# Graph layers on one core: scatter one-hots of the attention layer prebuilt in the propagation, and its combining step in float16

## The chip, the cores and the metric

The kernel runs on one core of one Trainium2 chip. The metric is the device time of one execution in microseconds (us); lower is better. An engine is named as the profile names it: PE (TensorE), PEld (its weight loads), DVE (VectorE), ACT (ScalarE), POOL (GpSimd), SP (SyncE, which here only issues DMAs).

## What is computed

Four graph layers, each on the layer norm and relu of the running `x` (3125 nodes of 64 features), over the same 53125 edges sorted by `dst`:

```python
h = relu(layernorm(x)); x = x + L0(h)   # K = 10 times: h' = 0.9 * norm * segsum(h[src] * norm[src]) + 0.1 * h0
h = relu(layernorm(x)); x = x + L1(h)   # attention per edge: 4 heads, exp(clip(q.k)), normalised per node, times v
h = relu(layernorm(x)); x = x + L2(h)   # segsum(h[src] * edge_weight) / deg, two 64x64 products
h = relu(layernorm(x)); x = x + L3(h)   # segsum(h[src] * sigmoid(edge_attr_64 @ ps_w)) * ci
```

## The kernel before, in words

The nodes lie as 25 tiles of 125 (`T`, `P`). A **flag** computed at run time picks the fast path, which all runs here take.

**Start.** DVE computes for each edge its tiles, its rank and its slot; meanwhile PE turns the 13.6 MB of edge features (L1285) and forms the logits of layer 3 from them (L1298), in 17 pieces. When the flag is known DVE sorts the edges into slots (L964 to L968, one round per tile, with PE L1341). At the end PE turns the 17 columns of logits back (L1361), ACT takes their sigmoid into `wpa` (L600, semaphore `pa_ready`), and POOL begins to place the pairs (edge weight, sigmoid) into `w_table` in HBM, with 425 indirect DMAs (L489). The table is read back (SP L425) before layer 2, after all placing is done (`w_placed`).

**Adjacency.** 25 rounds: DVE makes bf16 one-hots of sources and targets (L998, L1001), PE multiplies them (L1387), ACT copies the counts into `adj`, the 3125 x 3125 matrix in float16, which fills the arena. The target one-hots go to `ohd_table` in HBM for layers 2 and 3.

**Propagation (L0).** Ten iterations. `hl` holds each node's values as a float16 high part and a float16 low part, 128 columns. An iteration has seven chunks (`NCH`), six of 500 nodes and one of 125. For a chunk PE runs 25 matmuls, one per source tile (L1424), into the chunk's own PSUM bank; ACT copies the bank into `part` (L629, float32); PE *combines* the chunk one place behind (L1410): per tile of 125 nodes a float32 matmul, issued as two instructions, with the 125 columns of `part` as weights and `pair` (two identities on top of each other) as the moving operand. That adds high and low and turns them back to nodes on partitions. All combined tiles go through PSUM bank 7. DVE then makes the next `h`, high and low parts, in four instructions (L1074, L1077, L1079, L1081). Semaphores: `mains` (bank full), `mains_taken` (bank copied), `combined`, `sums_read` (bank 7 read by L1074), `hl_ready`. The combining of the seventh chunk stands inside the first chunk of the next iteration, after 12 of its matmuls.

**Edge layers (L1, L2, L3).** Software pipelines over 25 tiles plus four steps, each engine with its own order, written out in `edge_layer` and stepped by `tile_steps`. SP loads the source slots of a tile, spread to all partitions, into `rowbc` (L369, from `slot_rows`); DVE compares them with the lane number (L791) and so makes one-hots for the gather; PE gathers (L1237, L1242), the values are weighted, and PE scatters with one-hots of the other side (L1255). In the attention layer `rowbc` has two loads per tile, one for sources and one for targets, and one buffer for each. One step `s` of it on DVE is: L804 (products q times k, tile s-2), L791 (one-hot, tile s), L809 (logits, s-2), L791 (second one-hot, s), L815 (clip), L818 (low part of the message, s-3), L823 (weighted values, s-2), and L797, `ohd_of`: the scatter one-hots of tile s-2. On ACT it is: six of the 13 row copies (L528, tile s-1), the exponential (L536, after L815), seven more row copies, the high part (L546) and the sums (L564). PE's step is 13 groups of gathers for tile s-1, with the 26 scatter matmuls of tile s-4 behind the sixth group. Layers 2 and 3 read their scatter one-hots from `ohd_table` (L373) instead of computing them. The read waits until the scatter two tiles earlier has left its buffer, and stands in SP's one queue behind the step's loads of `rowbc`:

```python
if 2 in on and p != "l1":
    sp.wait_ge(S[p + "_scat"], d - 1)
    sp.dma_start(ohd_words[:, par], ohd_table[...])
```

## Time and profile before

| | us |
|---|---|
| Median of 3 runs | 1431.04 (1430.93 to 1431.52) |
| The profiled execution, its own time | 1421.67 |
| its span | 1420.0 |
| PE busy, share of the span | 1038.1, 73% |
| DVE busy | 958.2, 67% |
| POOL busy | 715.1, 50% |
| ACT busy | 566.7, 40% |
| Mean granted clock of PE | 0.826 |

The busy shares are means over stages with different limits. Stages of the span, by their first and last instructions: start and flag to 94 us, sorting to 205, adjacency to 335, propagation to 721, its residual and the next layer norm and products to 779, attention to 1067, layer 2 to 1275, layer 3 to the end.

### The profile page before, as it was taken

To read this page: it belongs to the slowest core of one execution; us is meant where nothing else is said; L and a number is where in the kernel's file an instruction comes from. 1 tells how busy PE (TensorE), PEld (TensorE's weight loads), DVE (VectorE), ACT (ScalarE), POOL (GpSimd) and SP (SyncE) were. 2 spreads that over 40 slices of the span, in tenths; PEclk is the share of its full clock that TensorE was granted. 3 is DMA by queue.
4 is the path that set the end of the run, shared out by engine and by line. 5 is a ranking of instruction groups with operands and counts; after the bars stand their busy time and mean duration, and the time that the engine had idled before them with its cause. 6 is when DMAs were issued, how large, how long until landed. Compare 5 with 4: busy or idle time off the path is not lost.

```text
span 1420.0 us, 32164 instructions
## 1 busy us (share of the span) xinstructions
PE 1038.1 (73%) x12016; PEld 802.3 (57%) x12016; DVE 958.2 (67%) x1175; ACT 566.7 (40%) x1381; POOL 715.1 (50%) x444
## 2 busy tenths in 40 slices
PE   4956567877999999999934677767762766646764
PEld 3635457763555555555524677766662666545664
DVE  7885779993223223223255999999997788558875
ACT  1321127662010101101113766666651777417773
POOL 1000018888787878787888899999940000000000
PEclk9977655567999999999967878888765999759997
DMA  7642006551000000000012544444411889418894
GB/s 153 137 102 70 23 14 208 180 190 30 2 2 2 1 1 1 1 1 2 2 51 52 192 145 145 161 153 156 156 67 50 330 321 344 159 42 328 326 334 147
DMA packets 61492, 169.86 MB, mean 120 GB/s; under 512 B 32531, under 2 KB 33331, under 8 KB 61437
## 3 DMA queue, kind: packets, MB, share of 16 engines
q1 hardware_dynamic: 45371, 154.59, 30.5%
q10 hardware_dynamic: 2465, 13.60, 4.1%
q0 software_dynamic: 13600, 0.92, 3.5%
q8 instruction: 36, 0.59, 0.2%
q14 instruction: 20, 0.16, 0.0%
HBM read 144.28 MB, written 24.33 MB: 119 GB/s over the span
## 4 chain that ended last, share of the span: by engine, by line
PE 39%; DVE 31%; issue 15%; DMA 9%; ACT 3%; DVEq 2%; SPq 1%; ACTq 0%
PE ps L1424 24%; DMA hl_room<-slot_rows 7%; PE ps L1410 4%; DVE arena L809 3%; DVE base_room L804 3%; PE ps L1237 3%; PE ps L1298 2%; PE ps L1255 2%; DVE hl_room L998 2%; DMA hl_room<-in_edge_attr_dram 2%; DVE arena L886 2%; PE ps L1285 2%; DVE h_room L823 2%; DVE arena L823 1%; ACT arena L561 1%
## 5 line engine op out<-in xcount | busy, mean ns | idle before, releaser
L489 POOL DMA_INDIRECT w_table<-wpa,slot_i x425 | 710.4, 1672 | 329.3 <-ACT wpa L600 200.1
L1237 PE MATMUL ps<-arena 125*128 125x64 f16 (+1 forms) x3900 | 257.2, 218 | 165.7 <-ACT arena L528 75.6
L1424 PE MATMUL ps<-arena,hl_room 125*128 125x500 f16 (+1 forms) x1750 | 345.1, 353 | 9.1 <-DVEq L1062 9.1
L1237 PEld LDWEIGHTS ps<-arena 125*128 125x128 bf16 x3900 | 189.8, 105 | 181.8 <-ACT arena L528 74.6
L1424 PEld LDWEIGHTS ps<-arena,hl_room 125*128 125x128 f16 x1750 | 161.6, 100 | 169.7 <-issue 13.2
L1074 DVE TENSOR_TENSOR h_room<-ps,coef 125x256 f32<-125x256 f32 (+1 forms) x70 | 27.7, 396 | 271.5 <-PE ps L1410 271.5
L629 ACT ACTIVATE part_room<-ps 128x500 f32<-128x500 f32 (+1 forms) x70 | 38.0, 543 | 349.7 <-PE ps L1424 349.7
L1255 PE MATMUL ps<-arena 128*128 128x128 f16 (+1 forms) x1950 | 142.7, 238 | 21.6 <-DVE arena L818 9.8
L1242 PE MATMUL ps<-arena 125*128 (+1 forms) x1300 | 149.6, 214 | 0.0
L1255 PEld LDWEIGHTS ps<-arena 128*128 128x128 bf16 x1950 | 131.2, 108 | 24.3 <-issue 22.0
L791 DVE TENSOR_SCALAR arena<-hl_room,lane 125x3328 bf16<-125x3328 bf16 x100 | 108.3, 1086 | 48.8 <-DMA hl_room<-slot_rows 47.5
L528 ACT ACTIVATE arena<-ps 128x384 f32<-128x384 f32 x325 | 131.0, 504 | 10.1 <-PE ps L1242 8.0
L1242 PEld LDWEIGHTS ps<-arena 125*128 125x128 bf16 x1300 | 124.5, 116 | 0.4
L554 ACT ACTIVATE arena<-ps,part_room 128x64 f32<-128x64 f32 x500 | 107.3, 343 | 16.4 <-PE ps L1237 16.3
L561 ACT ACTIVATE arena<-arena 128x1664 f16<-128x1664 f32 x50 | 79.5, 1591 | 61.9 <-DVE arena L841 56.0
L832 DVE TENSOR_TENSOR arena<-arena 128x1664 f16<-128x1664 f32 x50 | 94.4, 1888 | 14.6 <-ACT arena L561 14.5
L613 ACT ACTIVATE arena<-ps 125x500 f32 x150 | 79.7, 591 | 35.6 <-PE ps L1378 21.0
L582 ACT ACTIVATE part_room<-ps 128x500 f32<-128x500 f32 x68 | 34.6, 509 | 136.7 <-PE ps L1285 136.6
L1410 PEld LDWEIGHTS ps<-pair,part_room 128*125 128x125 f32 x500 | 64.7, 189 | 8.9 <-issue 0.7
L1298 PE MATMUL ps<-part_room,psw 128*26 128x125 f32 (+1 forms) x442 | 65.7, 291 | 1.0 <-ACT arena L574 0.8
L841 DVE TENSOR_TENSOR arena<-ps,part_room 128x512 f32<-128x512 f32 x100 | 64.2, 682 | 0.6 <-PE ps L1237 0.5
L1285 PE MATMUL ps<-ident,hl_room 125*128 125x125 f32 (+1 forms) x221 | 44.5, 326 | 26.7 <-DMA hl_room<-in_edge_attr_dram 18.8
(244 smaller groups left out, 1336.1 us busy)
## 6 DMA issues: line engine op xcount, KB each, us to landing
hl_room<-slot_rows SPq DMA_DIRECT2D x100, 832.0 KB, 5.6
arena<-ohd_table SPq DMA_DIRECT2D x50, 832.0 KB, 5.8
hl_room<-in_edge_attr_dram ACTq DMA_DIRECT2D x17, 750.0 KB
w_table<-wpa,slot_i POOLq DMA_INDIRECT x425
ohd_table<-hl_room SPq DMA_DIRECT2D x13, 448.0 KB, 2.6
ohd_table<-base_room SPq DMA_DIRECT2D x12, 448.0 KB, 2.6
ohd_table<-hl_room SPq DMA_DIRECT2D x13, 384.0 KB
ohd_table<-base_room SPq DMA_DIRECT2D x12, 384.0 KB
```

The lines of the kernel that those rows point to most:

```text
L489: pool.indirect_dma_start(w_table, bass.IndirectOffsetOnAxis(slot_i[:, u:u + 1], 0), wpa[:, u], None).then_inc(S[f"w_out{g % 2}"], 16)
L528: act.activation(G1[:, 1 - par, 2 * m:2 * m + 2, :], ps[:, m % RING, 0:2 * 3 * D].rearrange("p (c f) -> p c f", c=2), ACT.Copy).then_inc(S ...
L554: last = act.activation(msgf[:, par, c, :], ps[:, m, k * D:(k + 1) * D], ACT.Copy, scale=wsl[:, bass.ds((s - 2) * C + c, 1), 0 if p == "l2 ...
L561: act.activation(msg2[:, par, :, 0:D], msgf[:, par], ACT.Copy).then_inc(S[p + "_high"], 1)
L791: done = vec.tensor_scalar(ohT[:, par, e], rowbc[0:P, e if p == "l1" else par], lane[0:P, :], None, ALU.is_equal)
L832: vec.tensor_tensor(msg2[:, 1 - par, :, D:], msgf[:, 1 - par], msg2[:, 1 - par, :, 0:D], ALU.subtract).then_inc(S[p + "_low"], 1)
L1237: last = pe.matmul(ps[:, m % RING, o:o + b - a], ohT[:, par, 0, k * L:(k + 1) * L], rhs, start=(i == 0), stop=(i == 1))
L1242: last = pe.matmul(ps[:, m % RING, o + 2 * D:o + w], ohT[:, par, 1, k * L:(k + 1) * L], rhs, start=(i == 0), stop=(i == 1))
L1255: last = pe.matmul(ps[:, RING + par, 0:m1], ohd[par][:, k // 2, :, k % 2], msg1[:, par, k, :] if p == "l1" else msg2[:, par, k, :], start= ...
L1298: last = pe.matmul(ps[0:CJ + 1, 7, 0:P], psw2[0:w, at:at + CJ + 1], eaT[0:w, g % 2, k * P:(k + 1) * P], start=(block == 0), stop=(block == ...
L1410: last = pe.matmul(ps[0:P, 7, k * D:(k + 1) * D], part[:, odd, k * P:(k + 1) * P], pair[:, :], start=True, stop=True)
L1424: last = pe.matmul(ps[:, c, 0:w], hl[0:P, u, s, :], adj[:, s, c * CH * P:c * CH * P + w], start=(s == 0), stop=(s == T - 1))
```

## The change

- **Scatter one-hots of the attention layer**: DVE no longer makes them in that layer (`ohd_of` is gone). It makes them during the propagation, 50 halves, one behind each of the chunks 1 to 5 of every iteration, and SP writes them to a new table `ohs_table` in HBM. The attention layer reads them from there as layers 2 and 3 do. Their two buffers take the room of `xs` (the running `x`), so `x` is read again from HBM once the last half is written.
- **Turning in float16**: ACT writes the high part of a chunk's sums, scaled by 1/4096, as float16, DVE writes the low part (one instruction more per chunk, `low_sums`), and PE combines with two float16 matmuls per tile on 128 weight columns.
- **Weights placed from the flag on**: the logits of the first 250 of 425 edge columns are turned back and put through the sigmoid before the flag is known; POOL may place those at once, and the other 175 when the rest is ready.

```diff
@@ -30,6 +30,7 @@
+PSCALE = 4096.0
...
+        ohs_table = nc.dram_tensor("ohs_table", [T, L, CP * OW * 2], BF16).ap()
-        xs = sb("xs", [P, T, D])
+        xs_room = sb("xs_room", [L, KG[0] * OW])
+        xs = xs_room[0:P, 0:T * D].rearrange("p (t f) -> p t f", t=T)
-        part = part_room[:, 0:2 * CH * P].rearrange("p (a n) -> p a n", a=2)
+        part = part_room[:, 0:2 * CH * L].bitcast(F16).rearrange("p (a e n) -> p a e n", a=2, e=2)
-        pair = sb("pair", [L, D])
+        pair = sb("pair", [L, D], F16)
-        iota_h = sb("iota_h", [L, Q], F16)
+        iota_h = sb("iota_h", [L, OW], F16)
...
+        EARLY = EA_FLAG // 4
...
-                    if 2 in on and p != "l1":
+                    if 2 in on:
                         sp.wait_ge(S[p + "_scat"], d - 1)
-                        sp.dma_start(ohd_words[:, par], ohd_table[bass.ds(d - 2, 1)].rearrange("t p x -> p (t x)")
+                        sp.dma_start(ohd_words[:, par], (ohs_table if p == "l1" else ohd_table)[bass.ds(d - 2, 1)].rearrange("t p x -> p (t x)")
                                      ).then_inc(S[p + f"_ohd{par}"], 16)
                 tile_steps(sp, body)
                 sp.wait_ge(S[p + "_ohT"], T + free)
@@ -413,6 +421,16 @@
                     sp.wait_ge(S["table_ready"], n + 1)
                     sp.dma_start(g_table.rearrange("(t p) f -> p t f", p=P), h[:, :, :]).then_inc(S["table_in"], 16)
             with sp.If(way < 1):
+                with sp.Fori(0, T) as t:
+                    for half in range(2):
+                        a = sum(KG[:half]) * OW
+                        sp.wait_ge(S["ohs_made"], t * 2 + (half + 1))
+                        sp.dma_start(ohs_table[bass.ds(t, 1), :, a:a + KG[half] * OW].rearrange("t p x -> p (t x)"), ohs_words[half]
+                                     ).then_inc(S[f"ohs_out{half}"], 16)
+                for half in range(2):
+                    sp.wait_ge(S[f"ohs_out{half}"], 16 * (T + 1))
+                for a, b in SPLIT:
+                    sp.dma_start(xs[a:b, :, :], x.rearrange("(t p) f -> p t f", p=P)[a:b]).then_inc(S["x_back"], 16)
                 sp.wait_ge(S["rows_out"], 96)
                 sp.wait_ge(S["l0_done"], 1)
                 load_rows("l1", (1, 2))
@@ -472,17 +490,20 @@
...
                 pool.wait_ge(S["pa_ready"], 1)
                 pool.wait_ge(S["w_cleared"], 16)
+                assert EARLY * CJ % SU == 0
 
                 for g in range(J // SU):
+                    if g * SU == EARLY * CJ:
+                        pool.wait_ge(S["pa_ready"], 2)
...
             load_features(1)
             turned_features(0, EA_FLAG)
+            turned_logits(EARLY - 1)
+            act.wait_ge(S["z_back"], 1)
+            act.activation(wpa[:, 0:EARLY * CJ, 1], ps[0:P, 4, 0:EARLY * CJ], ACT.Sigmoid).then_inc(S["pa_ready"], 1)
             way = path(act)
             with act.If(way < 1):
                 act.activation(rep2[:, :, :], iota_h[:, 0:OW].unsqueeze(2).to_broadcast([L, OW, 2]), ACT.Copy).then_inc(S["rep_ready"], 1)
...
-                act.wait_ge(S["z_back"], 1)
-                act.activation(wpa[:, :, 1], ps[0:P, 5, 0:J], ACT.Sigmoid).then_inc(S["pa_ready"], 1)
+                act.wait_ge(S["z_back"], 2)
+                act.activation(wpa[:, EARLY * CJ:, 1], ps[0:P, 5, EARLY * CJ:J], ACT.Sigmoid).then_inc(S["pa_ready"], 1)
...
-                            act.activation(part[:, n % 2, 0:w], ps[:, c, 0:w], ACT.Copy).then_inc(S["mains_taken"], 1)
+                            act.activation(part[:, n % 2, 0, 0:w], ps[:, c, 0:w], ACT.Copy, scale=1 / PSCALE).then_inc(S["part_high"], 1)
                 act.wait_ge(S["rows_out"], 96)
...
                     done.then_inc(S[p + "_ohT" if e == ends - 1 else "l1_first"], 1)
-
-                def ohd_of(s, par):
-
-                    vec.wait_ge(S[p + "_scat"], s - 1)
-                    vec.tensor_tensor(ohd[par], nodes(C), pairs(sls_h[:, bass.ds((s - 2) * C, C)], C),
-                                      ALU.is_equal).then_inc(S[p + "_ohd"], 1)
...
@@ -1058,30 +1074,66 @@
                 one_hots_kept(vec)
                 fast(vec.tensor_copy(hl[0:P, 0, :, 0:D], h[:, :, :]))
                 fast(vec.tensor_tensor(hl[0:P, 0, :, D:], h[:, :, :], hl[0:P, 0, :, 0:D], ALU.subtract))
-                fast(vec.tensor_scalar(coef[:, :], rdeg[:, :], 1 - ALPHA, None, ALU.mult))
+                fast(vec.tensor_scalar(coef[:, :], rdeg[:, :], (1 - ALPHA) * PSCALE, None, ALU.mult))
+                vec.wait_ge(S["rows_out"], 96)
+                fast(vec.memset(part[:, :, :, CH * P:], 0.0))
+                vec.sem_inc(S["mains_taken"], NCH)
                 vec.sem_inc(S["hl_ready"], NCH)
                 vec.sem_inc(S["sums_read"], 1)
                 vec.wait_ge(S["base_ready"], 1)
-                with vec.Fori(0, K0 // 2) as i:
-                    for u in range(2):
-                        for c in range(NCH):
-                            n = u * NCH + c
-                            k = min(CH, T - CH * c)
-                            t = slice(CH * c, CH * c + k)
-                            turned = ps[0:P, 7, 0:k * D].rearrange("p (t f) -> p t f", t=k)
-                            vec.wait_ge(S["combined"], i * (2 * NCH) + (n + 3))
-                            vec.tensor_tensor(h[:, t, :], turned, coef[:, t].unsqueeze(2).to_broadcast([P, k, D]), ALU.mult
-                                              ).then_inc(S["sums_read"], 1)
...
+
+                def low_sums(i, n):
+                    c = n % NCH
+                    w = min(CH, T - CH * c) * P
+                    vec.wait_ge(S["part_high"], i * (2 * NCH) + (n + 1))
+                    vec.scalar_tensor_tensor(part[:, n % 2, 1, 0:w], ps[:, c, 0:w], 1 / PSCALE, part[:, n % 2, 0, 0:w],
+                                             ALU.mult, ALU.subtract).then_inc(S["mains_taken"], 1)
+
+                def new_nodes(i, n):
+                    u, c = n // NCH, n % NCH
+                    k = min(CH, T - CH * c)
+                    t = slice(CH * c, CH * c + k)
+                    turned = ps[0:P, 7, 0:k * D].rearrange("p (t f) -> p t f", t=k)
+
+                    vec.wait_ge(S["combined"], i * (2 * NCH) + (n + 3))
+                    vec.tensor_tensor(h[:, t, :], turned, coef[:, t].unsqueeze(2).to_broadcast([P, k, D]), ALU.mult
+                                      ).then_inc(S["sums_read"], 1)
+                    vec.wait_ge(S["sums_read"], i * (2 * NCH) + (n + 2))
+                    vec.tensor_tensor(h[:, t, :], h[:, t, :], base[:, t, :], ALU.add).then_inc(S["g_step"], 1)
+                    vec.wait_ge(S["g_step"], i * (4 * NCH) + (2 * n + 1))
+                    vec.tensor_copy(hl[0:P, 1 - u, t, 0:D], h[:, t, :]).then_inc(S["g_step"], 1)
+                    vec.wait_ge(S["g_step"], i * (4 * NCH) + (2 * n + 2))
+                    vec.tensor_tensor(hl[0:P, 1 - u, t, D:], h[:, t, :], hl[0:P, 1 - u, t, 0:D], ALU.subtract
+                                      ).then_inc(S["hl_ready"], 1)
+
+                def scatter_one_hots(t, k):
+                    j, half = k // 2, k % 2
+                    c, n = sum(KG[:half]), KG[half]
+                    vec.wait_ge(S[f"ohs_out{half}"], (t + j) * 16 + 16)
+                    vec.tensor_tensor(ohs_half[half], nodes(n), pairs(sls_h[:, bass.ds((t + j) * C + c, n)], n), ALU.is_equal
+                                      ).then_inc(S["ohs_made"], 1)
+                for half in range(2):
+                    vec.sem_inc(S[f"ohs_out{half}"], 16)
+
+                def two_iterations(i, more):
+                    for n in range(2 * NCH):
+                        u, c = n // NCH, n % NCH
+                        turn = c == NCH - 1
+                        if turn:
+                            new_nodes(i, n)
+                        if more or n + 1 < 2 * NCH:
+                            low_sums(i, n + 1)
+                        if not turn:
+                            new_nodes(i, n)
+                        if 1 <= c <= 5:
+                            scatter_one_hots(i * (T // (K0 // 2)), u * 5 + (c - 1))
+                low_sums(0, 0)
+                with vec.Fori(0, K0 // 2 - 1) as i:
+                    two_iterations(i, True)
+                two_iterations(K0 // 2 - 1, False)
                 vec.wait_ge(S["hl_ready"], (K0 + 1) * NCH)
                 vec.sem_inc(S["l0_done"], 1)
+                vec.wait_ge(S["x_back"], 32)
                 fast(vec.tensor_scalar(coef[:, :], std[:, :], 1.0 / GSCALE, None, ALU.mult))
                 fast(vec.tensor_tensor(h[:, :, :], h[:, :, :], per_node(coef), ALU.mult))
             with vec.Else():
...
+            pe.wait_ge(S["z_turned"], EARLY)
+            for c in range(EARLY):
...
@@ -1407,7 +1461,9 @@
                     pe.wait_ge(S["mains_taken"], n + (NCH + 1))
                     pe.wait_ge(S["sums_read"], n + 1)
                     for k in range(min(CH, T - CH * c)):
-                        last = pe.matmul(ps[0:P, 7, k * D:(k + 1) * D], part[:, odd, k * P:(k + 1) * P], pair[:, :], start=True, stop=True)
+                        for e in range(2):
+                            last = pe.matmul(ps[:, 7, k * D:(k + 1) * D], part[:, odd, e, k * P:k * P + L], pair[:, :],
+                                             start=(e == 0), stop=(e == 1))
                     last.then_inc(S["combined"], 1)
```

Two places where the order of the instructions counts. The first is **SP's queue in the attention layer's loop**, one step of it. Before (`hl_room<-slot_rows` is a load of `rowbc`):

```order
L369 ISA [waits l1_first]
L369 DMA hl_room<-slot_rows 128x3328
L369 ISA [waits l1_ohT]
L369 DMA hl_room<-slot_rows 128x3328
L368 REGISTER_ALU
```

and with the change:

```order
L377 ISA [waits l1_first]
L377 DMA hl_room<-slot_rows 128x3328
L377 ISA [waits l1_ohT]
L377 DMA hl_room<-slot_rows 128x3328
L380 REGISTER_ALU
L381 ISA [waits l1_scat]
L381 DMA arena<-ohs_table 128x3328
```

The next step's first load now stands behind a wait for a scatter on PE and behind a read of the same size.

The second is **DVE's queue in the propagation's loop**, the work behind one chunk of 500 nodes. Before:

```order
L1074 TENSOR_TENSOR h_room<-ps,coef 125x256 [waits combined]
L1077 TENSOR_TENSOR h_room<-h_room,base_room 125x256 [waits sums_read]
L1078 REGISTER_ALU
L1079 CAST hl_room<-h_room 125x4x64 [waits g_step]
L1080 REGISTER_ALU
L1081 TENSOR_TENSOR hl_room<-h_room,hl_room 125x4x64 [waits g_step]
```

and with the change:

```order
L1089 SCALAR_TENSOR_TENSOR part_room<-ps,part_room 128x500 [waits part_high]
L1098 REGISTER_ALU
L1099 TENSOR_TENSOR h_room<-ps,coef 125x256 [waits combined]
L1102 TENSOR_TENSOR h_room<-h_room,base_room 125x256 [waits sums_read]
L1103 REGISTER_ALU
L1104 CAST hl_room<-h_room 125x4x64 [waits g_step]
L1105 REGISTER_ALU
L1106 TENSOR_TENSOR hl_room<-h_room,hl_room 125x4x64 [waits g_step]
L1113 ISA [waits ohs_out1]
L1113 TENSOR_TENSOR xs_room<-rep,sls_h 128x1536
```

The low part of the following chunk stands ahead of the four instructions, and a half of one-hots behind them. Both can hold up what follows them on DVE.

## Rows read from the trace of the kernel before

**Rows 1.** By stretch: us, busy (instructions) by engine, granted clock, DMA share, GB/s

```profile
335.00:721.50 386.50, 384.18 (x2247) 216.41 (x2245) 109.31 (x280) 39.27 (x71) 308.49 (x257) 0.99 0.08 2
779.00:1067.00 288.00, 202.29 (x3200) 195.71 (x3197) 281.93 (x198) 188.00 (x421) 246.78 (x65) 0.79 0.43 146
```

**Rows 2.** Timeline, two chunks of the propagation: start us, us, engine, line, operation

```profile
506.80 5.45 PE L1424 MATMUL ps<-arena,hl_room 125*128 125x500 f16 x25
...
512.91 5.45 PE L1424 MATMUL ps<-arena,hl_room 125*128 125x500 f16 x25
```

**Rows 3.** Timeline, sorting: matmuls on 128 weight columns with 52 moving ones

```profile
170.25 1.16 PE L1341 MATMUL ps<-arena 125*128 125x52 bf16 x34
```

**Rows 4.** Timeline, from the sixth chunk's end into the next iteration

```profile
524.09 1.05 PEld L1410 LDWEIGHTS ps<-pair,part_room 128*125 128x125 f32 x8
...
524.50 0.59 ACT L629 ACTIVATE part_room<-ps 128x500 f32<-128x500 f32 x1 [5.52 <-PE ps L1424]
525.02 1.48 PEld L1424 LDWEIGHTS ps<-arena,hl_room 125*128 125x128 f16 x25
...
525.33 0.42 DVE L1074 TENSOR_TENSOR h_room<-ps,coef 125x256 f32<-125x256 f32 x1 [4.44 <-PE ps L1410]
...
526.57 0.43 DVE L1081 TENSOR_TENSOR hl_room<-h_room,hl_room 125x256 f16<-125x256 f32 x1
```

**Rows 5.** Groups by line: busy us, mean ns of one | idle before

```profile
L841 DVE TENSOR_TENSOR arena<-ps,part_room 128x512 f32<-128x512 f32 x100 | 64.2, 682 | 0.6 <-PE ps L1237 0.5
L998 DVE TENSOR_TENSOR hl_room<-rep,sl_h 128x1792 bf16<-128x1792 f16 (+1 forms) x50 | 50.9, 1018 | 5.2 <-PE ps L1378 2.8 <-ACT wpa L600 2.4
```

**Rows 6.** Timeline, SP at the kernel's end

```profile
1413.37 4.09 SPq L438 DMA_DIRECT2D out_dram<-xs  x2
```

**Rows 7.** The page's DMA part, an issue of one half: KB, us to landing

```profile
ohd_table<-hl_room SPq DMA_DIRECT2D x13, 448.0 KB, 2.6
```

**Rows 8.** Timeline, one step of the attention layer (DVE, ACT, two rows of PE)

```profile
904.29 0.39 PE L1237 MATMUL ps<-arena 125*128 125x128 f16 x2 [1.77 <-ACT arena L528]
...
906.20 1.89 DVE L804 TENSOR_TENSOR base_room<-arena 128x1664 f32<-128x1664 f32 x1
...
908.00 1.08 DVE L791 TENSOR_SCALAR arena<-hl_room,lane 125x3328 bf16<-125x3328 bf16 x1
...
908.13 2.32 PE L1255 MATMUL ps<-arena 128*128 128x136 f16 x26
...
910.80 1.08 DVE L791 TENSOR_SCALAR arena<-hl_room,lane 125x3328 bf16<-125x3328 bf16 x1
...
911.79 0.33 DVE L815 TENSOR_SCALAR arena<-arena,bound 128x104 f32<-128x104 f32 x1
...
912.83 2.76 ACT L528 ACTIVATE arena<-ps 128x384 f32<-128x384 f32 x7
...
915.74 1.89 DVE L797 TENSOR_TENSOR arena<-rep,sls_h 128x3328 bf16<-128x3328 f16 x1
...
917.55 1.89 DVE L804 TENSOR_TENSOR base_room<-arena 128x1664 f32<-128x1664 f32 x1
```

**Rows 9.** DMA issues of 850 to 1000 us: times, KB, median us to landing

```profile
hl_room<-slot_rows SPq DMA_DIRECT2D x26, 832.0 KB, 4.3
```

**Rows 10.** The same of 1120 to 1200 us, in layer 2

```profile
arena<-ohd_table SPq DMA_DIRECT2D x16, 832.0 KB, 5.7
hl_room<-slot_rows SPq DMA_DIRECT2D x16, 832.0 KB, 6.9
```

**Rows 11.** The chain that ended last, at the end of the sorting: start us, us

```profile
202.72 2.04 PE ps L1361 x17
...
204.78 0.55 ACT wpa L600
```

37 lines of the change are left out of this document (15 added, 22 removed).

## The prediction

> **What bounds the kernel now.** I read first the busy time by stretch, for a mean over the span hides that two stages have different limits. In the propagation PE is busy 384 of 386.5 us at a granted clock of 0.99, which is the upper of its two levels (2.4 GHz), with DVE at 28% [rows 1]: PE's own work sets that time. In the attention layer DVE is busy 282 of 288 us, PE 202 at a clock of 0.79, ACT 188: DVE sets it [rows 1]. Then I read the timeline of one piece of each. A chunk of 500 nodes returns every 6.11 us [rows 2]; 25 matmuls of 500 columns are 5.21 us at 2.4 GHz, so combining one chunk, with the change into it and out of it, costs 0.90 us. An attention step returns every 11.35 us, and DVE has no gap in it [rows 8].
>
> **Combining in float16.** An iteration combines 6.25 times four tiles, ten iterations 62.5 times: 62.5 x 0.90 = 56 us before. Afterwards there are two matmuls per tile, 64 columns each on 128 weight columns of 16 bits. The nearest row is the sorting's, 52 columns on 128: 34 in 1.16 us, 34 ns each with both ends [rows 3]. So 500 x 0.034 = 17 us, a saving of 39. From below: if the weight loads did not hide, each would cost what one float32 instruction costs now, 0.90 / 8 = 112 ns, and nothing were saved. I take the first, as its shapes and types are the same. The Trainium skill (TensorE: Matmul & The Clock Gate, Back-to-back issue gap) speaks against it: it gives about 81 ns per matmul in a stream of weight loads and matmuls of 128 columns. By that the 500 would be an estimated 40 us and the saving 16; the 34 ns of rows 3, for 52 columns, do not bear it out.
>
> **What the extra DVE work does to PE.** In a chunk DVE now has the low part (500 columns from PSUM; the nearest row is 682 ns for 512 [rows 5]), the four instructions (1.67 us from the first's start to the last's end [rows 4]) and behind five of seven chunks a half of one-hots (1018 ns in the mean for the same form [rows 5]): 3.4 us of 5.5, so in the long chunks it stays beside PE. It is different around the short chunk. Let T be the end of the sixth chunk's matmuls (524.09 in rows 4). ACT copies from T+0.41 to T+1.00 [rows 4]; the low part then lasts to T+1.7, the first of the four instructions to T+2.2, the fourth to T+3.4, the half of one-hots to T+4.5, the short chunk's low part (0.3, an estimate: a quarter of the 682 ns, and as much again for what does not shrink) to T+4.8, the first for chunk six to T+5.3, its fourth to T+6.5, another half to T+7.5, and the short chunk's four to T+8.5. PE has one combining (0.27) and the short chunk (1.48 [rows 4]) done by T+1.75, and must then wait for bank 7, read at T+2.2: 0.45 lost. Twelve matmuls of 0.21 later it waits for the same from T+4.95 to T+5.3: 0.35. Then twelve more, and the 25th matmul needs the short chunk's nodes: from T+7.9 to T+8.5, 0.65. That is 1.5 us an iteration, nine times: 13. Propagation: -39 + 13 = **-26 us**. Bounds: -39 if DVE turns out a little quicker, -10 if each wait were twice as long and the matmuls 44 ns.
>
> **The end of the propagation.** Before, DVE is done at T+6.0 in the last iteration (four instructions from T+1.24 [rows 4], four behind the next combining, and the short ones); now at T+8.5: +2.4. Then it waits for `x`. The last half is made at T+7.5, its write lands 2.6 us later [rows 7], and the read has the shape of the kernel's last write, which is issued at 1413.37 and ends the span at 1420.0, so 6.6 us [rows 6]. With 0.2 for semaphores `x` is back at T+16.9: DVE stands still for 8.4 us, and everything behind it with it, as PE, ACT and SP have nothing else to do. Bounds 5 (a read that lands quicker than the write) and 11. Together **+10.8 us**.
>
> **The attention layer.** L797 takes 1.81 us of a step (915.74 to 917.55 [rows 8]). Taken out, DVE needs 11.35 - 1.81 = 9.54 per step. First I ask who is late next. ACT's second seven copies begin 1.0 us behind L815's start and last 2.76, to 915.59 [rows 8], 9.39 behind the step's start at 906.20: L804 of the next step could start at 9.5. So ACT is just in time. The transfers are not. In SP's queue the next step's first load of `rowbc` now stands behind the wait for the scatter of this step on PE. PE starts its step when ACT has emptied the banks (904.29) and ends the scatter at 910.45 [rows 8], 6.2 later; the clock's mean there is 0.79 [rows 1], so other steps will be quicker: I take 5.7. Then come the read of the one-hots and, 0.6 us later, the load. A transfer keeps the DMA engines for 0.43 x 11.35 / 2 = 2.4 us [rows 1]. Alone such a load lands in 4.3 us [rows 9]; in layer 2, where both kinds alternate and the queue is never empty, in 6.9 [rows 10]. I take 6.5, so from the scatter's end to the landed load 0.1 + 0.6 + 6.5 = 7.2. The load is needed at L791, 1.80 into the next step, and from there to the step after next are 9.54 - 1.80 = 7.74 us of DVE and ACT. PE's start in that one closes the round, which so spans two steps: 2 x P = 5.6 + 7.2 + 7.74 = 20.5, P = 10.25. The second load, 2.4 us behind the first at most, is needed 2.8 later and binds less. Saving: 11.35 - 10.25 = 1.1 us, by 25 steps **-28 us**. Bounds: -45 (25 x 1.81, no wait) and 0 (below, the third rival). The DMA engines get three transfers of 832 KB per step in place of two, a share of 3 x 2.4 / 10.25 = 0.70, so they are not full.
>
> **The rest.** At the sorting's end 7 transposes in place of 17 (2.04 us) and a shorter sigmoid (0.55) [rows 11] stand on the chain; they would shrink by 1.2 and 0.3, and since a table load of ACT lies beside them I take **-1 us**. Before the flag PE and ACT have idle time for ten transposes and a sigmoid: zero, up to +1. POOL starts its 425 DMAs about 110 us earlier, and must be done some 22 us behind the end of attention, for `wsl`. In the propagation's stretch it now does 257, 1.2 us each, in attention's only 65, 3.8 us each [rows 1]: DVE's work holds it up. The one-hots will cost it some 35 in the propagation, the shorter stage 18, and I expect 30 to 50 more during the sorting; so it is done at about the same place in attention as before, late in it but ahead of the reading. Zero, up to +12.
>
> **Sum.** -26 + 10.8 - 28 - 1 = -44 against the profiled execution's 1421.7, 3.1%. The median of the runs is 9.4 us above it; I set the same difference against the median: 1431 - 44 = **1387**. A difference from no change can be told here from about 0.2%, 3 us.
>
> **Rivals.**
> - *The loads do not wait* (0.22). The scatter ends early since PE goes back to the upper clock level, or the load lands in 5. For it: the clock's mean is 0.79 [rows 1], so part of PE's 6.2 us ran at the lower level, and ACT is in time. Then P = 9.54, -45 in place of -28: 1370.
> - *The added DVE work hides entirely* (0.08): the waits at the short chunk come from sums of small guesses. -13: 1374.
> - *The three transfers share the DMA engines and land together, slower than before* (0.07). Each step then waits for all three: 3 x 2.4 and the 1.9 of a lone one that are not transfer, 0.7 for issues: 9.8; with PE at its lower level throughout, and the landing drawn out by half to 13: 2 x P = 6.1 + 13 + 7.74, P = 13.4, +51: 1466. It passes the time of before from P = 12.0 on, a landing 10.7 us behind the scatter, since the other terms come to -16. Against it: in layer 2, which has the same two kinds of transfer, the median landing is 6.9 and 5.7 [rows 10]. With 9.8 alone P = 11.6 and the kernel stands at 1421; I give that 0.1.
> - *The float16 weight loads do not hide* (0.05): at 112 ns the 39 us are not saved, though waits at the short chunk shrink: 1420. By the skill's 81 ns it would be an estimated 1410.
> - *The weights come late* (0.08): POOL gets no time during sorting, where DVE works without gaps, and is still placing when layer 2 asks: +12, 1399.
>
> **Chances.** 0.40 for the forecast, the rest as above. The likeliest case gives 1387. Range: down to 1366, which takes in the first two rivals with a little of their bounds, and up to 1412, which takes in late weights, a wait of 11 for `x` and most of the shared landing. Left out are the slow transfers, weight loads in the open, and 1348 (all terms at their best). Faster 0.93, the same 0.01, slower 0.06.
>
> **What would show it.** Right: in the propagation a chunk every 5.5 us, PE idle three times around the short chunk, by 1.5 us together; DVE idle about 8 us in front of L1137 (the former L1085), released by the read of `x`; attention steps of 10.2 us, with DVE waiting before the first of the two L791, released by a load of `slot_rows`; no wait of DVE for `wsl` ahead of layer 2. Wrong: steps of 9.5 us without a wait, or a DVE wait on ACT's copies; a chunk above 6 us; PE's granted clock below 0.95 in the propagation, which would mean that the short waits drag it to its lower level, a cost that no row of before lets me price.

## The result, and the profile after

| | before | changed |
|---|---|---|
| Median of 4 runs each, us | 1431.28 (1430.93 to 1435.31) | 1395.08 (1393.69 to 1399.33) |
| The profiled execution, its own time | 1421.67 | 1393.69 |
| its span | 1420.0 | 1392.0 |
| Mean granted clock of PE | 0.826 | 0.826 |

The ratio is 0.9746 (95% interval 0.9718 to 0.9774): 36 us faster, where 44 were forecast. The time of 1395 lies in the range, 8 us above the forecast. Two executions of kernels below, one of before_again with 1494.74 us and one of queue_all with 1927.06, were far slower than the others of the same kernel and are in no ratio or time given here.

By stretch of the changed kernel: us, busy (instructions) by engine (PE, PEld, DVE, ACT, POOL), granted clock, DMA share, GB/s; they answer to [rows 1]:

```profile
340.90:701.50 360.60, 351.48 (x2250) 173.97 (x2250) 188.78 (x393) 39.27 (x71) 289.61 (x234) 1.00 0.23 59
764.40:1033.60 269.20, 190.88 (x3250) 185.12 (x3250) 241.25 (x175) 190.57 (x426) 66.24 (x30) 0.82 0.66 241
```

PE now stands idle for 9 us in the propagation, where the rows show no gap before, and DVE for 28 in attention, where it had 10 in the same stretch (772.4 to 1067 us of the kernel before). To see what each stage gave, all kernels of this study are cut at the same five marks: PE's first matmul of the propagation, the end of its last combining, DVE's first one-hot of rows in attention, its first one in layer 2, the end. What each kernel is stands with its experiment below.

| kernel | ratio to before (95%) | up to the propagation | propagation | behind it | attention | layers 2, 3 |
|---|---|---|---|---|---|---|
| before | 1 | 333.4 | 386.4 | 52.6 | 320.9 | 326.6 |
| changed | 0.9746 (0.9718 to 0.9774) | 340.9 | 360.6 | 62.9 | 295.5 | 332.0 |
| before_again | 0.9976 (0.9946 to 1.0006) | 334.0 | 386.4 | 52.9 | 323.7 | 329.5 |
| after_again | 0.9739 (0.9697 to 0.9782) | 331.4 | 360.8 | 62.1 | 295.2 | 331.0 |
| comb_only | 0.9794 (0.9742 to 0.9846) | 333.7 | 355.0 | 48.5 | 320.9 | 331.1 |
| no_early | 0.9766 (0.9728 to 0.9803) | 335.5 | 358.5 | 63.0 | 298.1 | 331.9 |
| queue | 0.9603 (0.9566 to 0.9641) | 332.6 | 360.9 | 62.2 | 278.9 | 334.2 |
| queue_slots | 0.9571 (0.9530 to 0.9613) | 334.1 | 355.3 | 60.1 | 279.1 | 330.5 |
| queue_all | 0.9417 (0.9365 to 0.9469) | 334.7 | 355.4 | 60.7 | 279.9 | 311.7 |
| slots_last | 0.9491 (0.9450 to 0.9532) | 334.4 | 354.1 | 53.5 | 279.6 | 332.0 |
| before_queue | 0.9861 (0.9817 to 0.9904) | 339.5 | 386.4 | 53.8 | 322.0 | 311.2 |
| both | 0.9368 (0.9328 to 0.9407) | 343.9 | 355.2 | 53.4 | 280.9 | 310.2 |
| both_late | 0.9379 (0.9325 to 0.9432) | 337.8 | 355.8 | 54.1 | 280.4 | 311.5 |
| no_one_hots | 0.9639 (0.9601 to 0.9676) | 344.1 | 355.0 | 47.9 | 321.7 | 310.8 |

In the first two traces the stages differ by +7.5, -25.8, +10.3, -25.4 and +5.4: together the 28 us between the spans.

**The propagation.** PE's timeline around the turn of an iteration, answering to [rows 2, 4] (start us, us, engine, line, operation, and in brackets the idle time before it):

```profile
507.23 5.45 PE L1480 MATMUL ps<-arena,hl_room 125*128 125x500 f16 x25
512.52 0.40 PE L1465 MATMUL ps<-pair,part_room 128*128 128x64 f16 x8
512.75 5.45 PE L1480 MATMUL ps<-arena,hl_room 125*128 125x500 f16 x25
518.03 0.40 PE L1465 MATMUL ps<-pair,part_room 128*128 128x64 f16 x8
518.27 1.55 PE L1480 MATMUL ps<-arena,hl_room 125*128 125x125 f16 x25
520.01 0.39 PE L1465 MATMUL ps<-pair,part_room 128*128 128x64 f16 x8 [0.19 <-issue]
520.60 2.69 PE L1480 MATMUL ps<-arena,hl_room 125*128 125x500 f16 x12 [0.19 <-issue]
523.13 0.22 PE L1465 MATMUL ps<-pair,part_room 128*128 128x64 f16 x2
523.19 2.70 PE L1480 MATMUL ps<-arena,hl_room 125*128 125x500 f16 x12
526.24 2.07 PE L1480 MATMUL ps<-arena,hl_room 125*128 125x500 f16 x9 [0.35 <-DVE hl_room L1106]
```

A chunk returns every 5.52 us in place of 6.11, so combining one costs 5.52 - 5.21 = 0.31 in place of 0.90. Around the short chunk there are three gaps, and DVE's rows beside them say why the last one is there:

```profile
518.85 0.68 DVE L1089 SCALAR_TENSOR_TENSOR part_room<-ps,part_room 128x500 f16<-128x500 f32 x1 [2.26 <-ACT part_room L652]
519.45 0.41 DVE L1099 TENSOR_TENSOR h_room<-ps,coef 125x256 f32<-125x256 f32 x1
...
521.11 0.95 DVE L1113 TENSOR_TENSOR xs_room<-rep,sls_h 128x1536 bf16<-128x1536 f16 x1
521.98 0.28 DVE L1089 SCALAR_TENSOR_TENSOR part_room<-ps,part_room 128x125 f16<-128x125 f32 x1
...
524.21 1.08 DVE L1113 TENSOR_TENSOR xs_room<-rep,sls_h 128x1792 bf16<-128x1792 f16 x1
525.22 0.22 DVE L1099 TENSOR_TENSOR h_room<-ps,coef 125x64 f32<-125x64 f32 x1
...
525.96 0.22 DVE L1106 TENSOR_TENSOR hl_room<-h_room,hl_room 125x64 f16<-125x64 f32 x1
```

With T = 518.03, the end of the sixth chunk's matmuls, DVE works from T+0.8 to T+8.2 without a gap, two halves of one-hots (L1113) among it, and PE's 25th matmul waits for the last of it. Over the nine turns the first gap is 0.19 us each time, the second (0.19) is there in three, and the third is 0.34 to 0.62, 0.47 in the mean.

**Behind the propagation.** SP issues the reading back of `x`, DVE waits for it:

```profile
706.89 3.57 SPq L433 DMA_DIRECT2D xs_room<-in_x_dram  x2
```

```profile
704.24 0.23 DVE L1106 TENSOR_TENSOR hl_room<-h_room,hl_room 125x64 f16<-125x64 f32 x1
715.59 0.18 DVE L1137 TENSOR_SCALAR coef<-std 125x25 f32<-125x25 f32 x1 [11.12 <-DMA xs_room<-in_x_dram]
...
721.48 1.82 DVE L1147 TENSOR_TENSOR xs_room<-xs_room,h_room 125x1600 f32<-125x1600 f32 x1 [3.86 <-issue]
```

Both pieces of `x` are there 8.7 us behind the start of the issue. Of the 11.1 us of waiting 1.8 come back two instructions later, where DVE stood still before too: 3.86 in place of 5.64 us. That instruction, the adding of `x`, first in the kernel before, then in comb_only (below), where the gap is not there:

```profile
729.21 1.82 DVE L1095 TENSOR_TENSOR xs<-xs,h_room 125x1600 f32<-125x1600 f32 x1 [5.64 <-issue]
```

```profile
693.49 1.82 DVE L1131 TENSOR_TENSOR xs_room<-xs_room,h_room 125x1600 f32<-125x1600 f32 x1 [0.60 <-DVE h_room L1122]
```

The DMA part of the kernel before, from 721.5 to 729.5 us, has a packet of a queue that the profile calls instruction:

```profile
q14 instruction: 1, 0.01, 0.3%
```

All twelve traces with a gap of 3.2 us or more here have such a packet of q14 some 2 us ahead of the adding of `x`; the two with 0.60 us, comb_only and no_one_hots, have none. So this gap goes with a piece of the program being loaded. That the load causes it, and why those two kernels have none there, was not tried.

**Attention.** DVE's L840 of three steps and the first L814 between them, then the chain of waits in the same place:

```profile
894.81 1.89 DVE L840 TENSOR_TENSOR h_room<-arena 128x1664 f32<-128x1664 f32 x1
...
904.35 1.89 DVE L840 TENSOR_TENSOR arena<-arena 128x1664 f32<-128x1664 f32 x1
...
909.03 1.09 DVE L814 TENSOR_SCALAR arena<-hl_room,lane 125x3328 bf16<-125x3328 bf16 x1 [0.99 <-DMA hl_room<-slot_rows]
...
914.97 1.89 DVE L840 TENSOR_TENSOR h_room<-arena 128x1664 f32<-128x1664 f32 x1
```

```profile
900.53 1.64 PE ps L1304 x26
902.32 0.33 SPq L381
903.21 5.80 DMA hl_room<-slot_rows
```

The scatter on PE ends at 902.17, and only then does SP issue the read of the one-hots (L381) and behind it the row load, which lands at 909.01: 6.8 us from the scatter's end. One step of two waits for it: 9.54 us, then 10.62. Over the whole stretch DVE waits 20.8 us for rows, in 12 places; before it was 5.5, in 3.

POOL issues its last scatter of weights in the first third of attention, not late in it:

```profile
838.31 1.19 POOL L510 DMA_INDIRECT w_table<-wpa,slot_i  x1 [0.30 <-issue]
```

### The profile page after: what moved, and what is told of

The parts are those of the page before. It is cut to its first block, busy times and chain, and to the rows that moved or that the text cites. A ratio compares the mean times of both kernels' runs of the same rounds, so it can differ in the third digit from the quotient of the medians.

```text
span 1392.0 us, 32611 instructions
## 1 busy us (share of the span) xinstructions
PE 990.4 (71%) x12016; PEld 747.9 (54%) x12016; DVE 999.0 (72%) x1271; ACT 568.9 (41%) x1383; POOL 618.8 (44%) x444
## 4 chain that ended last, share of the span: by engine, by line
PE 39%; DVE 24%; DMA 16%; issue 13%; ACT 5%; DVEq 1%; SPq 1%; ACTq 0%; another core or an unknown queue 0%
PE ps L1480 20%; DMA hl_room<-slot_rows 13%; PE ps L1289 4%; PE ps L1304 4%; PE ps L1347 2%; DMA hl_room<-in_edge_attr_dram 2%; DVE arena L902 2%; ACT arena L549 2%; PE ps L1441 2%; PE ps L1334 2%; DVE arena L826 1%; DVE base_room L1017 1%; DVE xs_room L1113 1%; DVE hl_room L1017 1%; DVE arena L848 1%
## 5 line engine op out<-in xcount | busy, mean ns | idle before, releaser
L510 POOL DMA_INDIRECT w_table<-wpa,slot_i x425 | 614.1, 1445 | 219.8 <-issue 219.8
L1289 PE MATMUL ps<-arena 125*128 125x64 f16 (+1 forms) x3900 | 248.4, 216 | 160.6 <-DVE arena L857 72.6
L1289 PEld LDWEIGHTS ps<-arena 125*128 125x128 bf16 x3900 | 188.6, 105 | 175.3 <-DVE arena L857 68.7
L1480 PEld LDWEIGHTS ps<-arena,hl_room 125*128 125x128 f16 x1750 | 155.2, 97 | 176.6 <-DVEq L1080 9.7
L652 ACT ACTIVATE part_room<-ps 128x500 f16<-128x500 f32 (+1 forms) x70 | 38.0, 543 | 322.9 <-PE ps L1480 290.6
L1089 DVE SCALAR_TENSOR_TENSOR part_room<-ps,part_room 128x500 f16<-128x500 f32 (+1 forms) x70 | 43.5, 622 | 164.9 <-ACT part_room L652 129.3
L814 DVE TENSOR_SCALAR arena<-hl_room,lane 125x3328 bf16<-125x3328 bf16 x100 | 108.7, 1090 | 69.5 <-DMA hl_room<-slot_rows 68.2
L1304 PE MATMUL ps<-arena 128*128 128x128 f16 (+1 forms) x1950 | 139.3, 235 | 19.7 <-DVE arena L835 8.5
L1304 PEld LDWEIGHTS ps<-arena 128*128 128x128 bf16 x1950 | 127.7, 106 | 22.2 <-issue 22.2
L1294 PE MATMUL ps<-arena 125*128 (+1 forms) x1300 | 138.8, 208 | 0.0
L1294 PEld LDWEIGHTS ps<-arena 125*128 125x128 bf16 x1300 | 117.0, 110 | 0.3
L582 ACT ACTIVATE arena<-arena 128x1664 f16<-128x1664 f32 x50 | 79.6, 1591 | 66.1 <-DVE arena L857 58.0
L1014 DVE TENSOR_TENSOR hl_room<-rep,sl_h 128x1792 bf16<-128x1792 f16 (+1 forms) x50 | 51.1, 1022 | 6.7 <-PE ps L1432 5.2
```

The lines of the kernel that those rows point to most:

```text
L510: pool.indirect_dma_start(w_table, bass.IndirectOffsetOnAxis(slot_i[:, u:u + 1], 0), wpa[:, u], None).then_inc(S[f"w_out{g % 2}"], 16)
L582: act.activation(msg2[:, par, :, 0:D], msgf[:, par], ACT.Copy).then_inc(S[p + "_high"], 1)
L814: done = vec.tensor_scalar(ohT[:, par, e], rowbc[0:P, e if p == "l1" else par], lane[0:P, :], None, ALU.is_equal)
L1289: last = pe.matmul(ps[:, m % RING, o:o + b - a], ohT[:, par, 0, k * L:(k + 1) * L], rhs, start=(i == 0), stop=(i == 1))
L1294: last = pe.matmul(ps[:, m % RING, o + 2 * D:o + w], ohT[:, par, 1, k * L:(k + 1) * L], rhs, start=(i == 0), stop=(i == 1))
L1304: last = pe.matmul(ps[:, RING + par, 0:m1], ohd[par][:, k // 2, :, k % 2], msg1[:, par, k, :] if p == "l1" else msg2[:, par, k, :], start= ...
```

## The experiments

Lines are those of each kernel: the first one-hot of rows in attention, L791 before and L814 in the changed kernel, is L818 in queue.

### What of the two traces is the change

before_again and after_again are the two kernels unchanged.

> The changed kernel as it is. Two stages that I had costed at nothing came out longer in its first trace: the start (sorting begins at 123.1 us in place of 119.3, the adjacency stage lasts 127.9 us in place of 123.4) and layers 2 and 3 (332.0 in place of 326.6 from the first L814 of layer 2 to the end). Theory A, the change causes them: they come back here within 1 us each. Theory B, they are the scatter of single executions: at least one of the three lies nearer to the numbers of before. Both: 1393 to 1397 us.

> The kernel before, unchanged, for a second trace of it: layers 2 and 3 lasted 326.6 us in the one trace so far, and 331.0 to 334.2 in all five kernels that hold parts of the change. Theory A, something that all of them share (xs lying in the larger xs_room, other places in memory, more DMA descriptors) lengthens layers 2 and 3 by 5 us: 326 to 328 here. Theory B, the first trace was a lucky one: 330 to 333 here. Propagation in both: 386.4.

**Measured.** The start is in the main scatter, theory B of after_again: sorting begins at 119.67, the adjacency stage lasts 123.1 us. The adjacency stage by stretch (columns as above) in before, changed, after_again and before_queue:

```profile
210.00:333.40 123.40, 90.47 (x1301) 84.72 (x1302) 111.77 (x180) 82.79 (x153) 102.98 (x68) 0.56 0.54 178
```

```profile
213.00:340.90 127.90, 92.25 (x1300) 86.39 (x1301) 112.56 (x181) 83.09 (x153) 107.48 (x68) 0.52 0.52 172
```

```profile
208.30:331.40 123.10, 91.42 (x1300) 85.58 (x1301) 112.00 (x181) 82.81 (x153) 102.97 (x67) 0.53 0.54 179
```

```profile
211.60:339.50 127.90, 93.10 (x1300) 87.21 (x1300) 112.42 (x180) 83.20 (x153) 107.49 (x68) 0.51 0.52 172
```

Over all 14 traces it takes 123.0 to 123.7 us in nine and 127.9 to 130.6 in five, and one of the five, before_queue, holds nothing of the change. Layers 2 and 3 are less clear: 329.5 in the second trace of before lies near theory B, and still all seven kernels with a part of the change and the old order of reads lie above both traces of before (330.5 to 334.2). A part of the 5 us may be real; its cause stays open. With the new order of reads (below) nothing of it is seen: 311.2 in before_queue, which holds nothing of the change, and 310.2 to 311.7 in the four kernels with it.

### Combining alone: comb_only

```diff
-                        if 1 <= c <= 5:
-                            scatter_one_hots(i * (T // (K0 // 2)), u * 5 + (c - 1))
...
+                        ohd_of(s, par)
...
-        EARLY = EA_FLAG // 4
```

> Of the change only the float16 combining is left: scatter one-hots are computed by DVE in the attention layer again, weights are placed from the end of the sorting on. Theory A, the waits of PE around the short chunk come from the one-hot halves queued on DVE: 62.5 combinings save 0.59 each, 37 us, and only the first of three waits stays (0.45 x 9 = 4), so the propagation lasts 353 us (386.4 before, 360.6 with the whole change), and the kernel takes 1431 - 33 = 1398. Theory B, the waits come from the low part and float16 combining itself: the propagation stays at 360, the kernel at 1405. Both: attention steps of 11.35 us as before.

**Measured.** The propagation takes 355.0 us, two from theory A's 353 and five from B's 360, so theory A for the most part; the ratio is 0.9794, 29 us, where 33 were expected. An iteration returns after 34.91 and 35.27 us in turns, 35.09 in the mean, against 38.25 before and 35.67 in the changed kernel. Seven combinings (six and a quarter) save 6.25 x 0.59 = 3.7 of the 38.25; so 0.5 us of an iteration are lost to the low part and the conversions, and 0.6 to the halves. The turn of an iteration in this kernel shows what is left of the gaps: the first one, and at three of the nine turns 0.2 us of issue ahead of the twelve (not at this one):

```profile
544.82 1.55 PE L1462 MATMUL ps<-arena,hl_room 125*128 125x125 f16 x25
546.56 0.39 PE L1447 MATMUL ps<-pair,part_room 128*128 128x64 f16 x8 [0.19 <-DVE h_room L1089]
546.79 2.70 PE L1462 MATMUL ps<-arena,hl_room 125*128 125x500 f16 x12
```

Attention takes 320.9 us, as before (320.9 and 323.7): its gain in the changed kernel is that of the one-hots. The part ahead of it takes 48.5, 4 less than before, and the gap in front of the adding of `x`, 0.60 in place of 5.64 us, is more than the whole of that.

### The order in SP's queue: queue

```diff
-                    if 2 in on:
+                    if p != "l1" and 2 in on:
...
+                    if p == "l1" and 3 in on:
+                        sp.wait_ge(S["l1_scat"], d - 2)
+                        sp.dma_start(ohd_words[:, 1 - par], ohs_table[bass.ds(d - 3, 1)].rearrange("t p x -> p (t x)")
+                                     ).then_inc(S[f"l1_ohd{1 - par}"], 16)
```

> The whole change, with one thing moved: in SP's queue the read of the stored one-hots of a tile is issued one step later, behind a scatter that is then done, so the loads of slot_rows no longer stand behind a wait for PE. Theory A (the forecast's): steps fall from 10.1 to 9.54 us, DVE's waits for slot_rows in attention from about 20 us to under 5, the kernel to 1395 - 14 = 1381. Theory B, the three transfers of 832 KB share the DMA engines (0.66 of their time in attention), and the loads come late whatever the order: waits stay above 12 us, the kernel at 1390 to 1395. Theory C, the read now comes late for PE: PE waits for ohs_table in front of L1304 by over 0.5 us a step, and the kernel is slower than 1395.

**Measured.** Theory A: 1369.29 us beside 1385.6 of the changed kernel on the same chip, 16 less, all of it in attention (278.9 us for 295.2). SP's queue over one step, first of after_again (one of those that wait), then of queue:

```profile
894.09 0.33 SPq L381 DMA_DIRECT2D arena<-ohs_table  x1
894.97 0.85 SPq L377 DMA_DIRECT2D hl_room<-slot_rows  x2
```

```profile
893.24 3.11 SPq L377 DMA_DIRECT2D hl_room<-slot_rows  x2
896.60 0.33 SPq L385 DMA_DIRECT2D arena<-ohs_table  x1
```

The two row loads of a step now go out over 3.1 us, each when its room is free, and not in a bunch of 0.85 us behind the read. DVE's L844 returns after 9.62 and 9.55 us, and between 756 and 1000 us DVE waits for `slot_rows` 5.7 us in place of 20.0, in two places, none of them here (before the change it was 5.5 in three):

```profile
888.30 1.89 DVE L844 TENSOR_TENSOR arena<-arena 128x1664 f32<-128x1664 f32 x1
...
897.92 1.88 DVE L844 TENSOR_TENSOR h_room<-arena 128x1664 f32<-128x1664 f32 x1
...
907.47 1.88 DVE L844 TENSOR_TENSOR arena<-arena 128x1664 f32<-128x1664 f32 x1
```

Theory B falls: with the same bytes in less time (DMA share 0.69 between 745 and 1000 us, 249 GB/s, for 0.66 and 238 in after_again) the waits are gone. Theory C falls too: no wait of PE for `ohs_table` is in the trace. The Trainium skill (DMA: Bandwidth & Descriptors, Anatomy of one DMA) has the rule behind it: DMA engines don't wait on semaphores, the issuing sequencer does. The trace agrees: in the changed kernel a row load lands 6.8 us behind the end of a scatter that it doesn't need.

### The same order in layers 2 and 3: queue_all, before_queue

```diff
-                    if 2 in on:
-                        sp.wait_ge(S[p + "_scat"], d - 1)
-                        sp.dma_start(ohd_words[:, par], (ohs_table if p == "l1" else ohd_table)[bass.ds(d - 2, 1)].rearrange("t p x -> p (t x)")
-                                     ).then_inc(S[p + f"_ohd{par}"], 16)
+                    if 3 in on:
+                        sp.wait_ge(S[p + "_scat"], d - 2)
+                        sp.dma_start(ohd_words[:, 1 - par], (ohs_table if p == "l1" else ohd_table)[bass.ds(d - 3, 1)].rearrange("t p x -> p (t x)")
+                                     ).then_inc(S[p + f"_ohd{1 - par}"], 16)
```

> As the kernel with the moved read and halves behind chunks 0 to 4, and the read of the kept one-hots is moved behind the next step's rows in layers 2 and 3 too. DVE waits for slot_rows 42 to 47 us there. Theory A, these waits come from the order in SP's queue as in attention: they fall below 15 us and the kernel by 25 us or more against its pair. Theory B, a step of layer 2 or 3 with two transfers of 2.4 us in some 5.5 us is near what the DMA engines give, and PE needs the one-hots at the start of its step: the wait moves to PE (L1304 for ohd_table) or stays, and the kernel gains under 5 us or loses.

> The kernel before with one edit, the read of the kept one-hots of layers 2 and 3 moved one step later in SP's queue. Theory A, the order in the queue cost the kernel before as much as the changed one: layers 2 and 3 fall from 327 to 330 us to about 310, the kernel by 18 us, a ratio of 0.987. Theory B, the gain of the same edit (20 us) hung on the other parts of the change: under 5 us, a ratio above 0.996.

**Measured.** queue_all takes 1341.96 us (the median of three) beside 1362.98 of its pair, queue_slots below, from which it differs by this edit alone; layers 2 and 3 take 311.7 us for 330.5. The kernel before gains the same from the same edit, theory A of its run: 311.2 us there, 19 us in all, ratio 0.9861. DVE's waits from 1030 to 1360 us (us in total, times, the longest), in queue_slots:

```profile
DVE arena L818 <- DMA hl_room<-slot_rows: 44.6, 36, 3.4
DVE arena L852 <- ACT arena L586: 15.9, 22, 2.1
```

and in queue_all:

```profile
DVE arena L848 <- ACT arena L582: 36.4, 48, 1.7
...
DVE arena L814 <- DMA hl_room<-slot_rows: 3.3, 1, 3.3
```

41 us of waiting for rows go and 20 us of waiting for ACT come: half of the gain is handed to the next one in line, ACT's conversion L582. So 19 us are gained in these layers, 21 by the times, where theory A said 25 or more; the waits fell as A said, and what A left out is the wait for ACT.

### Where the halves stand: queue_slots, slots_last

queue_slots:

```diff
-                        if 1 <= c <= 5:
-                            scatter_one_hots(i * (T // (K0 // 2)), u * 5 + (c - 1))
+                        if c <= 4:
+                            scatter_one_hots(i * (T // (K0 // 2)), u * 5 + c)
```

> The kernel with the moved read, and the one-hot halves now behind chunks 0 to 4 of an iteration in place of 1 to 5, so none stands on DVE between the low part and the nodes of the sixth chunk and the short chunk's. Theory A (the forecast's): PE's wait for the short chunk's nodes goes (0.46 us a time), an iteration takes 35.2 us in place of 35.67, and the last half is made 3 us earlier at the end, so x comes 3 us earlier: 9 x 0.46 + 3 = 7 us less than the kernel with the moved read alone, 1362. Theory B, the waits come from the low part and its order alone: iterations stay at 35.7 and 3 us are gained: 1366.

slots_last, against queue_slots:

```diff
-                        if c <= 4:
-                            scatter_one_hots(i * (T // (K0 // 2)), u * 5 + c)
+                        if more and c <= 4:
+                            scatter_one_hots(i * (T // (K0 // 2)), u * 5 + c)
+                        if not more and (u == 0 or c <= 2):
+                            scatter_one_hots(i * (T // (K0 // 2)), n)
```

> As the kernel with the moved read and halves behind chunks 0 to 4, but the last pair of iterations makes its ten halves behind the seven chunks of its first iteration and the first three of its second, so that x can be read back before the propagation ends. Theory A: the read back of x lands before DVE has done the last nodes; DVE's wait in front of L1137 (some 8 us in its pair) goes, and one more stall of up to 1.5 us comes at the turn between the two: 6 us less than its pair. Theory B, the time behind the propagation is set by something else (the issue time of 3.6 us in front of the add, PE): under 2 us are gained.

**Measured.** Theory A for queue_slots: an iteration takes 35.1 us, as long as in comb_only, so the halves cost PE nothing any more, and the propagation is 5.6 us shorter, a little more than the 4 expected. The part behind it is 2.1 shorter, where 3 were expected. In slots_last the wait for `x` is gone:

```profile
690.64 1.83 DVE L1144 TENSOR_TENSOR h_room<-h_room,coef 125x1600 f32<-125x1600 f32 x1
698.34 1.82 DVE L1153 TENSOR_TENSOR xs_room<-xs_room,h_room 125x1600 f32<-125x1600 f32 x1 [5.87 <-issue]
```

The part behind the propagation takes 53.5 us, as before the change (52.6 and 52.9). Against the changed kernel that is 9 us less, not the whole 11 of the wait, and against its pair, whose wait was 8.8 us, it is 6.6, since 5.87 us of issue are back. By time slots_last is 10.4 us below its pair, by the propagation and the part behind it 7.8; the rest is within the scatter of runs. Theory A expected 6.

### Weights late: no_early, both_late

```diff
-                    if g * SU == EARLY * CJ:
-                        pool.wait_ge(S["pa_ready"], 2)
...
-            act.activation(wpa[:, 0:EARLY * CJ, 1], ps[0:P, 4, 0:EARLY * CJ], ACT.Sigmoid).then_inc(S["pa_ready"], 1)
```

> The whole change but the early placing of weights (POOL starts behind the sigmoid at the sorting's end, and so does PE with all 17 transposes). Theory A, POOL's early scatters hold up the edge feature loads and lengthen the start: sorting begins at 119.3 again and adjacency lasts 123.4; the 95 scatters that POOL no longer has done by then cost nothing, since it ends before 1030 us: 1395 - 7.5 + 1 = 1388. Theory B, the start does not depend on it: 1396. Theory C, the early placing was needed: POOL is still placing when layer 2 asks at about 1055, and DVE waits for wsl: 1400 or more.

> As the kernel with all three, without the early placing of weights (POOL starts at some 205 us in place of 96). Theory A, POOL still ends before attention does (972 us in the kernel with late weights so far, attention's last rows at 967 in the faster one), so only the 2 to 3 us come back that attention takes longer while POOL works beside it: 1336. Theory B, it ends too late for wsl: DVE or SP waits in front of layer 2, 1345 or more. Theory C, no difference: 1333.

**Measured.** no_early is at 0.9766 beside the 0.9739 of the changed kernel on the same chip, both_late at 0.9379 beside 0.9368: the intervals overlap. So placing early can't be told from placing late, which is theory C of both_late. Of no_early's theories C falls, as no wait for `wsl` came, and A and B can't be told apart: its adjacency stage takes 123.7 us, but that of after_again, with early placing, takes 123.1. Over all 14 traces sorting begins at 119.7 to 123.2 us in the eight kernels with early placing (121.7 in the mean) and at 118.4 to 120.6 in the six without (119.5), and adjacency at 211.4 and 210.6 in the mean. So early placing seems to cost some 2 us ahead of the sorting and to give back 1.5 of them in it, less than single traces scatter. POOL's last scatter in both_late:

```profile
1006.96 2.37 POOL L506 DMA_INDIRECT w_table<-wpa,slot_i  x1 [0.30 <-issue]
```

SP waits 22.2 us for it ahead of the read of `wsl`, which it issues at 1010.78; DVE's first instruction on `wsl` stands at 1024.16, behind no wait for it. Some of the cover is left, but not much.

### All together: both, no_one_hots

both is queue_all with slots_last; no_one_hots is both with the edit of comb_only on the one-hots alone.

> The changed kernel with all three: reads moved in all three layers, halves behind chunks 0 to 4, and in the last pair of iterations behind seven chunks and three. Theory A, the gains lie in different stages and add up: 1343 - 10 = 1333. Theory B, an earlier or a shorter stage brings POOL's placing of weights or the transfers into the way: above 1338.

> As the kernel with all three, but the scatter one-hots of attention are computed on DVE again, and x is not read back. Theory A (the forecast's for this part, with the queue mended): attention takes 315 us in place of 280, the propagation and the part behind it as long as with the one-hots within 2 us, so 35 us more: 1368. Theory B, the one-hots' move is worth less than DVE's 1.81 us a step, since the third transfer slows what is left: 15 us or less.

**Measured.** both takes 1341.09 us, 0.9368 of before, the fastest kernel here beside both_late. By its time alone that is above theory B's 1338, but the kernel before is 5 us slower beside it than beside queue_all. Against queue_all (0.9417) the expected 10 us, 0.007 of the ratio, came to 0.005, within the intervals; from the propagation's start to the end it is 999.7 us for 1007.7, so 8 us are gained, and its trace has the long adjacency stage (130.6 us), as has that of no_one_hots (130.5). Without the moved one-hots the kernel is at 0.9639, 38 us slower: the two parts from the propagation's end to layer 2 take 369.6 us in place of 334.3, and nothing else changes by over 1 us. By the sum, 35 us, that is theory A, but its parts were expected otherwise. Attention takes 321.7 us for 280.9, 41 more and not 35, which is 1.6 us a step where L797 takes 1.81; and the part ahead of it takes 47.9 for 53.4, 5.5 less and not the same within 2, as the gap in front of the adding of `x` is 0.60 us in place of 5.78.

## Why the prediction was right, point by point

- **What bounds it: right.** PE sets the propagation, and taking 0.59 us off a chunk took it off the stage. DVE sets attention, and its step fell to 9.54 us as soon as nothing else held it.
- **Combining in float16: right.** 62.5 x 0.59 = 37 us were saved where 39 were forecast, 39 ns a matmul for the 34 of [rows 3]. The 81 ns of the Trainium skill (TensorE: Matmul & The Clock Gate, Back-to-back issue gap) would make a combining of eight an estimated 0.65 us; the page has them for 128 moving columns, there are 64 here, and the trace has 0.31 for all eight.
- **What the DVE work does to PE: right in kind, a third too large.** An iteration lost 3.7 - 2.6 = 1.1 us, not 1.5. DVE's order came as laid out, but two of the three gaps were smaller: 0.19 in place of 0.45 before the combining, and 0.47 in the mean in place of 0.65 at the 25th matmul. The one of 0.35 foreseen twelve matmuls after the first, for bank 7, did not come; at three of nine turns 0.19 us of issue stand ahead of those twelve, and what that is stays open. The gaps come to 0.7 us an iteration; the other 0.4 of the 1.1 is in no gap and stays open too. That the propagation came to -25.8 for -26 so closely is luck: the errors of the two terms and of the last chunk's cancelled.
- **The reading of x: right in kind, a size off.** Forecast 8.4 us of waiting; measured 11.1 and 10.3. The step that failed is "the read has the shape of the kernel's last write": it took 8.7 us from its issue, not 6.6. What the sum left out are attention's first row loads, which go out inside that time; in slots_last, where none is near, the read's transfer is all but over 6.9 us behind its issue (last section). Another 0.7 us is the last half's write, 3.3 us from the half made to the read's issue for 2.6. (The Trainium skill, DMA: Bandwidth & Descriptors, Anatomy of one DMA, gives a fit of 2 us and bytes by 436 GB/s for DMAs that GpSimd issues; SP issues this read, and by that fit it would take an estimated 3.8 us, which the trace does not bear out.) DVE's 1.8 us of issue that this hides were not in the sum, so the part grew by 10.3 and 9.2 us for 10.8: again two errors that cancel.
- **Attention: right, with its mechanism.** From PE's start of a step to the scatter's end are 5.7 us (896.50 to 902.17), from there to the landed load 6.8 for 7.2, and the round spans two steps: 20.2 us for 20.5. (That sum has 5.6 where its text takes 5.7; with 5.7 it gives 26 us and not 28.) The stage gave 25.4 us, and 27.0 in the mean of two traces each, for 28. The experiment with the read moved took the rest, 16 us, where 9.54 a step would give 17. The rival of the loads that do not wait fell; so did those of shared transfers.
- **POOL: right by the sum, wrong on the way.** "The one-hots will cost it some 35 in the propagation" failed: it issued 234 scatters in 360.6 us there, a scatter in 1.54 us, and 257 in 386.4 before, one in 1.50. And DVE without L797 held it up far less: with L797 one scatter of three takes 7.54 us or more in attention, without it the 30 scatters had a mean of 2.2. So it ended at 839 us and not late in attention.
- **What was costed at nothing.** The start came out 7.5 us longer where -1 was forecast, layers 2 and 3 5.4 longer: 14 of the 16 us between the forecast and the two traces. The first is for the most part scatter between executions, shown by the second trace (2.0 us shorter than before); in the mean over all traces adjacency begins 0.8 us later with early placing, where -1 was forecast. Of the second a part is left open. Against the median of runs the sum missed by 8 us.

## What to carry to other kernels

A queue issues in its own order (SP's did here): before a load goes into it behind a wait, ask who finishes that wait and what stands behind it. A read that is needed a step later can wait for a thing that is then long done; here that one edit was worth 16 us in attention and 19 in layers 2 and 3, the latter in the kernel before as well. Work moved into an idle engine's time is free only where it does not stand between two things that another engine alternates with: behind chunks 1 to 5 the halves cost 0.6 us an iteration, behind 0 to 4 nothing, and a buffer borrowed from data that comes back late costs most of the return, here 9 us. A gain of a stage can be paid for in part by its neighbour (41 us in attention, 5.5 of them back ahead of it): compare kernels by the sum of both.
